# Mixing stage of a four-stage kernel: score products of four heads sent together, and small steps moved between ScalarE, VectorE and GpSimd

## What is computed

```python
x = x + attn(xn) + ffn(xn)
```

```python
nx = _rmsnorm(X, g1)                       # X * rsqrt(mean(X*X) + 1e-6) * g1
Q = (nx @ Wq.T).reshape(B, S, H, dk).transpose(0, 2, 1, 3)    # H = 4, dk = 32
Kc = nx @ Wkc.T                            # one key of 32 for all heads
Vc = nx @ Wvc.T
scores = jnp.einsum('bhsd,btd->bhst', Q, Kc) * scale
attn = jax.nn.softmax(scores, axis=-1)
out = jnp.einsum('bhst,btd->bhsd', attn, Vc)
out = out.transpose(0, 2, 1, 3).reshape(B, S, d) @ Wo.T
X = X + out
```

## Time and profile before

| | |
|---|---|
| median of 3 runs | 2581.19 us (2569.83 to 2581.81) |
| profiled execution: its own time | 2584.21 us |
| profiled execution: its span, first to last instruction | 2582.4 us |
| `mix`, first scores to last row's end | 1708 to about 2130 us |
| one loop row of `mix` | 26.00 us |
| busy over the whole span | PE 89%, DVE 74%, ACT 61%, POOL 40% |

### The profile page before, as it was taken

How to read it: one execution, slowest core, us unless ns; L and a number is a source line. 1 busy time by engine, 2 the same in 40 slices (tenths; PEclk the granted TensorE clock), 3 DMA queues, 4 the chain that set the end, 5 groups by cost and what they waited for, 6 DMA issues and landing times. The chain is left out here.

```text
span 2582.4 us, 102624 instructions
## 1 busy us (share of the span) xinstructions
PE 2293.3 (89%) x37544; PEld 1609.2 (62%) x37544; DVE 1905.0 (74%) x3734; ACT 1584.7 (61%) x3954; POOL 1038.4 (40%) x1350
## 2 busy tenths in 40 slices
PE   5773599999999999999998999869999996999999
PEld 3441477767767677677676777646666664666665
DVE  5663488878878788788787888637676764777777
ACT  3442477778777777777777777637777772232322
POOL 5664445545554555455445554300000002333332
PEclk9886799999999999999999999959999997999999
DMA  6887345544544455455444554300010101101010
GB/s 191 271 271 205 87 108 120 115 108 110 122 107 111 102 124 112 106 116 123 104 115 105 121 112 105 67 25 26 24 37 24 37 25 58 37 24 37 24 37 16
DMA packets 568188, 243.42 MB, mean 94 GB/s; under 512 B 462278, under 2 KB 531526, under 8 KB 563142
## 3 DMA queue, kind: packets, MB, share of 16 engines
q1 hardware_dynamic: 567750, 237.52, 36.7%
HBM read 134.13 MB, written 103.29 MB: 92 GB/s over the span
## 5 line engine op out<-in xcount | busy, mean ns | idle before, releaser
L886 ACT ACTIVATE a_probs<-a_bank_s,a_neg_max 128x512 f32<-128x512 f32 x1024 | 694.6, 684 | 184.2 <-DVE a_neg_max L821 180.1
L821 DVE TENSOR_REDUCE a_neg_max<-a_bank_s 128x2 f32<-128x1024 f32 x512 | 627.0, 1225 | 56.0 <-ACT a_probs L886 3.7
L673 PE MATMUL a_bank_pt<-a_ident,a_probs 128*128 128x128 f32 x4096 | 573.1, 283 | 8.5 <-issue 2.6
L673 PEld LDWEIGHTS a_bank_pt<-a_ident,a_probs 128*128 128x128 f32 x4096 | 445.1, 143 | 116.4 <-issue 79.1
L866 ACT ACTIVATE a_probs_t<-a_bank_pt 128x512 f32<-128x512 f32 x512 | 305.9, 597 | 201.4 <-PE a_bank_pt L673 196.0
L807 DVE COPY a_probs_t<-a_bank_pt 128x512 f32<-128x512 f32 x512 | 350.1, 684 | 32.4 <-PE a_bank_pt L673 24.5
L662 PE MATMUL a_bank_s<-a_k,a_q 48*32 48x512 bf16 (+15 forms) x4096 | 274.1, 290 | 94.0 <-DMA a_kl<-scr_parts 65.0
L699 PE MATMUL a_bank_o<-a_probs_t,a_v 128*32 128x32 f32 (+2 forms) x15872 | 305.8, 228 | 2.0 <-issue 2.0
L699 PEld LDWEIGHTS a_bank_o<-a_probs_t,a_v 128*32 128x32 f32 x15872 | 245.8, 112 | 58.8 <-ACT a_probs_t L866 48.4
L662 PE MATMUL a_bank_s<-a_kl,a_q 48*32 48x204 bf16 (+14 forms) x3840 | 241.4, 266 | 23.6 <-ACT a_probs L886 19.1
L800 DVE TENSOR_TENSOR a_bank_s<-a_bank_s,a_win 128x144 f32<-128x144 f32 (+2 forms) x640 | 164.2, 275 | 125.9 <-PE a_bank_s L662 113.1
(11 more groups left out here) (161 smaller groups left out, 3600.1 us busy)
## 6 DMA issues: line engine op xcount, KB each, us to landing
scr_probs<-a_probs SPq DMA_DIRECT2D x256, 144.0 KB, 5.2
a_raw<-scr_qr SPq DMA_DIRECT2D x256, 96.0 KB
scr_qr<-p_qr SPq DMA_DIRECT2D x64, 320.0 KB, 2.9
a_feat<-scr_probs SPq DMA_DIRECT2D x256, 78.0 KB
scr_parts<-p_sp SPq DMA_DIRECT2D x144, 128.0 KB, 2.9
a_left<-scr_probs SPq DMA_DIRECT2D x256, 64.0 KB, 2.5
a_q<-scr_parts SPq DMA_DIRECT2D x32, 192.0 KB
a_k<-scr_parts SPq DMA_DIRECT2D x32, 192.0 KB
```

The costliest lines, as they stand in the source:

```text
L673: ins = nc.tensor.transpose(b_pt[bank_of(job)][:, 0, t * P:(t + 1) * P], probs[(u - 1) % 4][:, j, MAX_REL + t * P:MAX_REL + (t + 1) * P], ...
L821: nc.vector.tensor_reduce(neg_max[:, 2 * pair:2 * pair + 2], b_s[:, 2 * pair:2 * pair + 2, :], AX.X, ALU.max, negate=True).then_inc(max_ok, 1)
L886: nc.scalar.activation(probs[u % 4][:, j, MAX_REL:MAX_REL + S], b_s[:, j, :], ACT.Exp, bias=neg_max[:, j:j + 1], accum_out=sums[:, t, j, u ...
```

## The change

In the words of the code:

- TensorE, line 1198 on: a step is now the transposes of heads 0 and 1 of the tile before, then the score products of all four heads one after the other, then the transposes of heads 2 and 3, `attended` and the small jobs. The four products wait once, for all four exponentials of the tile before. Each raises `s_ps` (before, one of two did).
- VectorE: the two copies now stand ahead of the maxima (copy of head 1, maximum of heads 0 and 1, copy of head 3, maximum of heads 2 and 3). The function `highest` holds the same reading of two heads in one instruction as before. The readings of `inv`, Q and V come to it from ScalarE. The scaling `nx = xn * rms` leaves it. The mean square plus epsilon moves from step 1 to the end of step 0.
- ScalarE: a step is now both copies (heads 0 and 2) and then the four exponentials. The four squares stand in step 0 between the two copies, ahead of the exponentials.
- GpSimd: the widening of the inverse sums now comes first, then the power, then `nx = xn * rms` as one instruction on 128 x 512.
- SyncE is as it was.

```diff
@@ TensorE @@
                     for pair in ((0, 1), (2, 3)):
-                        if own:
-                            for h in pair:
-                                need(pe, exp_ok, b, 4 * NT, 4 * (u - 1) + h + 1)
-                                ins = nc.tensor.matmul(b_s[:, h, :], Q[s][h * D2:(h + 1) * D2, u * P:(u + 1) * P],
-                                                       K[s][h * D2:(h + 1) * D2, :], start=True, stop=True)
-                            ins.then_inc(s_ps, 1)
+                        if own and pair[0]:
+                            need(pe, exp_ok, b, 4 * NT, 4 * u)
+                            need(pe, max_ok, b, 2 * NT, 2 * u)
+                            for h in range(H2):
+                                nc.tensor.matmul(b_s[:, h, :], Q[s][h * D2:(h + 1) * D2, u * P:(u + 1) * P],
+                                                 K[s][h * D2:(h + 1) * D2, :], start=True, stop=True).then_inc(s_ps, 1)
                         if (own and u) or (old and not u):
@@ VectorE @@
+            def highest(b, u, pair):
+
+                v.wait_ge(s_ps, b * H2 * NT + H2 * u + 2 * pair + 2)
+                nc.vector.tensor_reduce(neg_max[:, 2 * pair:2 * pair + 2], b_s[:, 2 * pair:2 * pair + 2, :],
+                                        AX.X, ALU.max, negate=True).then_inc(max_ok, 1)
+
                 for u in range(NT):
                     for pair in range(2):
-                        if own:
-                            v.wait_ge(s_ps, b * 2 * NT + 2 * u + pair + 1)
-                            need(v, exp_ok, b, 4 * NT, 4 * (u - 1) + 2 * pair + 2)
-                            nc.vector.tensor_reduce(neg_max[:, 2 * pair:2 * pair + 2], b_s[:, 2 * pair:2 * pair + 2, :],
-                                                    AX.X, ALU.max, negate=True).then_inc(max_ok, 1)
                         if (own and u) or (old and not u):
                             job = (u, "probs", 2 * pair + 1)
                             job_done(v, b, job)
                             need(v, av_ps, b, NT, u - 2)
                             nc.vector.tensor_copy(probs_t[(u - 1) % 2][:, 2 * pair + 1, :], b_pt[bank_of(job)][:, 0, :]
                                                   ).then_inc(pt_ev[bank_of(job)], 1)
+                        if own:
+                            need(v, exp_ok, b, 4 * NT, 4 * (u - 1) + 2 * pair + 2)
+                            highest(b, u, pair)
-                    if u == 1 and new:
-                        need(v, rms_ok, b, 1, 2)
-                        if kind != "lead":
-                            job_done(v, b - 1, (1, "nx", 0))
-                        for t in range(NT):
-                            ins = nc.vector.tensor_scalar(nx[:, t, :], xn[:, t, :], rms[:, t:t + 1], None, ALU.mult)
-                        ins.then_inc(nx_ok, 1)
+                    if u == 1 and old:
+                        job = (1, "inv", 0)
+                        job_done(v, b, job)
+                        need(v, att_ok, b, 1, 0)
+                        nc.vector.tensor_copy(inv_t[:], b_pt[bank_of(job)][:, 0, :]).then_inc(pt_ev[bank_of(job)], 1)
...
                     if u == 2 and new:
+                        job = (2, "q", 0)
+                        job_done(v, b, job)
+                        need(v, s_ps, b, H2 * NT, 0)
+                        nc.vector.tensor_scalar(Q[1 - s][:], b_pt[bank_of(job)][:, 0, :], D2 ** -0.5, None, ALU.mult
+                                                ).then_inc(pt_ev[bank_of(job)], 1)
...
+                    if u == 3 and new:
+                        job = (3, "v", 0)
+                        job_done(v, b, job)
+                        need(v, av_ps, b, NT, 0)
+                        nc.vector.tensor_copy(V[1 - s][:], b_pt[bank_of(job)][:, 0, 0:NT * D2]
+                                              .rearrange("p (t d) -> p t d", d=D2)).then_inc(pt_ev[bank_of(job)], 1)
@@ GpSimd @@
+                if new:
+                    need(g, ms_ok, b, 1, 2)
+                    nc.gpsimd.tensor_tensor(rms[:], rms[:], pows[:].to_broadcast([P, NT]), ALU.pow).then_inc(rms_ok, 1)
+                    need(g, rms_ok, b, 1, 2)
+                    if kind != "lead":
+                        job_done(g, b - 1, (1, "nx", 0))
+                    nc.gpsimd.tensor_tensor(nx[:], xn[:], rms[:].rearrange("p (t o) -> p t o", o=1)
+                                            .to_broadcast([P, NT, E]), ALU.mult).then_inc(nx_ok, 1)
@@ ScalarE @@
                 for u in range(NT):
+                    if (own and u) or (old and not u):
+                        read_probs(b, u, 0)
+                    if u == 0 and new:
+
+                        need(act, xn_in, b, 16, 32)
+                        need(act, ms_ok, b, 1, 1)
+                        for t in range(NT):
+                            need(act, sq_ok, b, NT, NT + t)
+                            nc.scalar.activation(square[:], xn[:, t, :], ACT.Square, accum_out=mean_sq[:, t:t + 1]
+                                                 ).then_inc(sq_ok, 1)
+                    if (own and u) or (old and not u):
+                        read_probs(b, u, 2)
+                    if not own:
+                        continue
                     for pair in range(2):
...
                         for j in (2 * pair, 2 * pair + 1):
                             if u or old:
                                 job_done(act, b, (u, "probs", j))
                             nc.scalar.activation(probs[:, j, :], b_s[:, j, :], ACT.Exp, bias=neg_max[:, j:j + 1],
                                                  accum_out=sums[s][:, u, j:j + 1]).then_inc(exp_ok, 1)
```

More of the change, by code:

```diff
@@ L1241, in row @@
                                                   ).then_inc(pt_ev[bank_of(job)], 1)
-                        if u == 1 and pair == 0 and new:
-                            need(v, sq_ok, b, NT, 2 * NT)
-                            need(v, rms_ok, b, 1, 1)
-                            need(v, nx_ok, b, 1, 1)
-                            nc.vector.tensor_scalar(rms[:], mean_sq[:], 1.0 / E, RMS_EPS, ALU.mult, ALU.add
-                                                    ).then_inc(ms_ok, 1)
+                        if own:
+                            need(v, exp_ok, b, 4 * NT, 4 * (u - 1) + 2 * pair + 2)
+                            highest(b, u, pair)
                     if u == 0 and old:
@@ L1294, in row @@
                 own, old, new = parts(kind)
-                if new:
-                    need(g, ms_ok, b, 1, 2)
-                    nc.gpsimd.tensor_tensor(rms[:], rms[:], pows[:].to_broadcast([P, NT]), ALU.pow).then_inc(rms_ok, 1)
                 if old:
@@ L1311, in _, with read_probs @@
             act.wait_ge(const_in, N_IN)
+            def read_probs(b, u, j):
+                job = (u, "probs", j)
+                job_done(act, b, job)
+                need(act, av_ps, b, NT, u - 2)
+                nc.scalar.activation(probs_t[(u - 1) % 2][:, j, :], b_pt[bank_of(job)][:, 0, :], ACT.Copy
+                                     ).then_inc(pt_ev[bank_of(job)], 1)
             def row(b, s, kind):
@@ L1315, in row @@
                 for u in range(NT):
-                    for pair in range(2):
-                        if (own and u) or (old and not u):
-                            job = (u, "probs", 2 * pair)
-                            job_done(act, b, job)
-                            need(act, av_ps, b, NT, u - 2)
-                            nc.scalar.activation(probs_t[(u - 1) % 2][:, 2 * pair, :], b_pt[bank_of(job)][:, 0, :],
-                                                 ACT.Copy).then_inc(pt_ev[bank_of(job)], 1)
-                        if not own:
-                            continue
+                    if (own and u) or (old and not u):
+                        read_probs(b, u, 0)
+                    if u == 0 and new:
+                        need(act, xn_in, b, 16, 32)
[8 more added lines that the diff above has]
+                        continue
+                    for pair in range(2):
                         act.wait_ge(max_ok, b * 2 * NT + 2 * u + pair + 1)
```

33 lines of the change are left out of this document (6 added, 27 removed).

## The result

The changed kernel took 2608.29 us (median of 4 runs, 2606.66 to 2614.65), against 2577.66 for the kernel before in the same session (4 runs, 2569.83 to 2581.81). The ratio is 1.0121, interval 1.0093 to 1.015: the change made the kernel slower by 1.2%. Against the 2581.19 of before that is 2612; the prediction said 2617, within 2583 to 2650.

A forecast was written before the change was run, and what follows sets the result against it. TensorE was taken to bound the kernel. The profiled 2584.2 us, plus 10 without the clock and 26 for falls of TensorE's clock, gave 2620; less 3.0 by which that execution exceeded the median, 2617, range 2583 to 2650.

The forecast's parts named there:

- Four heads for the price of two: Mixing stage scores: four heads' products run side by side in 1.06 us, taking 4.2 us from TensorE in each row.
- The bare chain: From a step's scores through maxima, copy and exponentials on VectorE and ScalarE to the next scores: 5.77 us.
- Steps 1 to 3 at 2.4 GHz: Loop row steps where transposes wait for bank readings of `nx`, K and the residual: 6.14, 6.74 and 6.53 us.
- Step 0 and the late load: Squares wait for `xn`, loaded behind the store and landing at 2.68, and hold up the exponentials: step 0 takes 7.65 us.
- The clock: TensorE's gap in step 0 drops it to 1.2 GHz in 8 rows of 10, 2.5 us each: +26 us.
- My ends for one fall: Cost in step 1: 1.9 us if only its first 4 us are slow, 4.4 if the whole step is.
- The rival in which the clock holds: Same waits in the loop rows, but the gap is too short to lower TensorE's clock: 2591 us, chance 0.25.
- Row 0: First row of the mixing stage, at 1.2 GHz: shorter scores but also the chain's waits, -3 us, between -6 and 0.
- The last row: Three steps grow towards 5.8 us and the end behind them is shorter: 0, between -2 and +2 us.
- saves nothing: Moving the four `nx` scalings from VectorE to GpSimd gains no time, since VectorE did them while TensorE was the bound.
- that alone is 0.6: Step 2: Q's reading, formerly on ScalarE beside K's, now stands ahead of K's on VectorE, costing 0.6 us.
- The faster rival: The load of `xn` doesn't hold up the squares: step 0 5.77, row 25.18, clock holds, 2567 us, chance 0.12.

The follow-up runs named there:

- the pair experiment: Scores again in pairs, each pair ahead of its transposes, against the changed kernel with the early load; 2588.82 us, ratio 1.0014.
- the early load: Changed kernel, but SyncE sends the load of `xn` as soon as `nx` is worked out, ahead of the store; 2566.34 us, ratio 0.994.
- the later load: Changed kernel, but the load of `xn` is sent behind the load of `xo`, which waits for the last store; 2640.27 us, ratio 1.0218.

## Why the prediction came out as it did

**The forecast was right in sign, mechanism and size** (2617 forecast; ratio 1.0121, which is 2612 on the 2581.19 of before). Point by point:

- **Four heads for the price of two: right.** 1.07 from start to start, against 1.06 forecast. The smaller gain that the Trainium skill states ("TensorE: Matmul & The Clock Gate", "Part 3: Packing small matmuls — row/col tiling", 3.07 times for four) would give 1.38, an estimate; this trace doesn't agree with it. The gain of 4.2 us is there from start to start, and it is mostly waited away, as said: 3.0 of it by the pair experiment.
- **The bare chain: right.** 5.77 forecast, 5.76 in row 1, and 5.76 in every row with the early load. Row 1 is 25.13, forecast 25.18.
- **Steps 1 to 3 at 2.4 GHz: right within 0.1.** 6.14, 6.74 and 6.53 forecast; 6.12, 6.66 and 6.59 measured. Step 2 is 0.08 shorter because the next reading follows Q's by 0.60, not 0.66.
- **Step 0 and the late load: right.** 7.65 forecast, 7.81 measured, and the experiment that moves the load takes exactly this away. The load itself landed when I said, 2.65 behind the scores on average, against 2.68. In this my issue was early: I took 1.32 behind the residual, which holds in every second row; in the others it is 1.60 (1896.68 to 1898.29 above), and their step 0 is 7.85 to 8.04 against 7.62 to 7.87. A landing 2.6 and not 2.7 behind the issue, and a residual 1.40 and not 1.34 ahead of the scores, made up for it. What was missing is the way from the landing to the first square: I gave it 0.02 (2.68 to 2.70), and it is 0.17 in all 13 rows.
- **The clock: right in kind, both factors off.** I said a fall in 8 rows of 10 at 2.5 each, 2.0 a row. It fell in 13 of 13, and step 1 grew by 1.90 on average (8.02 - 6.12): by 2.38 in the seven rows with a slow stretch of 6.8 us (mean 8.50) and by 1.34 in the six with one of 3.4 us (mean 7.46). My ends for one fall, 1.9 and 4.4, were both too high for the short ones, and my share of rows was too low. The two errors nearly cancel, which is luck: +26 forecast, 13 x 1.90 = +24.7 measured. The rival in which the clock holds was wrong; of the earlier trace rows the first stretch was the nearer one, as I took it to be.
- **Row 0: sign right, size not.** -3 forecast (-6 to 0), -8.3 measured. I assumed that the row would run at 1.2 GHz as it did before. But with four heads together it doesn't stay there. Row 0 took 33.3, 31.3 and 32.8 us in the three kernels with pairs (before, the same with the early load, and the pairs experiment), in all of which the clock was back at 2.4 GHz only at 1729 or later; it took 24.6 to 25.9 in the eight with four heads together, in all of which it was back by 1724, in the kernel after by 1711. Why it comes back so much earlier no run shows.
- **The last row: 0 forecast, -0.5 measured.**
- **Two side claims fell.** That taking `nx` off VectorE "saves nothing" holds for the kernel before, where TensorE is the bound; once the chain is the bound, the place tried for it on VectorE costs 1.0 us a row. And "that alone is 0.6" about Q standing ahead of K on VectorE was wrong as a statement on the change: the other place for it, behind the exponentials of ScalarE, costs 0.61 more. I had compared with a chain in which Q's reading disappears, not with one in which it is somewhere else.
- **The faster rival** put the price of a load in time at 2567 for the kernel. It was not what happened, but it was worked out rightly: made true by the experiment, it gives a row of 25.13 (25.18 forecast) and a ratio of 0.994, 2566 on the 2581 of before.

In sum, for the stage: forecast +10 without the clock and +26 for it, 36. Measured +30.4, of which 24.7 is the clock. The rest is 13 x (27.18 - 26.00) = +15.3 (27.18 is the mean row with 6.12 as its step 1), less 0.97, 8.31 and 0.46: +5.6, where the forecast had 13.8, less 0.8 and 3: +10. The waits came out 1.5 dearer and row 0 5.3 cheaper. So the sum was 5.6 too high, about as much as row 0 alone was off.

## What to carry to other kernels

Work taken from the engine that bounds a kernel is worth only what the chain behind it allows: write that chain down as start-to-start times, step by step, from the rows at hand; here it gave each step to within 0.2 us at the full clock before anything ran. A late load costs nothing while its reader comes later still; here it became the whole loss when the reader was moved ahead of work that the emptied TensorE was waiting for. So look at what stands ahead of each load on its own queue (here a store), and send the load as soon as its buffer is free. Price an idle gap of TensorE twice, once as a wait and once for the slower clock behind it: here 2.05 and 1.9 us.

## What the runs showed of the hardware that I had not expected

- The clock fell without any long gap. With the squares behind the exponentials TensorE was idle for 1.15 and then for 0.94 us with 1.14 of work between them, and in each of rows 1 to 14 it was granted 1.2 GHz before the second of these was over; with one idle time of 1.15 and 1.73 of 2 us busy behind it, it kept 2.4 GHz from row 1 to the end of the stage (the early load).
- Useless work can pay: 64 more small products in a gap of 2.67 us made a row 1.7 us shorter, because what follows ran at 2.4 GHz.
- A slow stretch does not cost in proportion to its length. With the later load each one was 6.8 us long, and step 1 grew by only 1.42 (7.54 - 6.12); in the kernel after the stretches of the same length cost 2.38. In the first kernel 3.6 us of the stretch were over when the scores of step 1 came (1894.4 to 1897.95), in the second 0.7 (1817.1 to 1817.8).
- A busy TensorE did not get its clock back at once. In the kernel before with the early load the clock fell in row 0 at 1713.6 and stayed down for 17.1 us, of which TensorE was busy for 15.45; with four heads together the falls in row 0 lasted 3.4 or 6.8 us.
